# Attention, router and the first expert layer on one core: convolution weights loaded apart, router indices first, second-layer weights made at the end, attention order written out anew

## What is computed

```python
x = x + _L0_conv_ref(_ln_c(x), ...)      # attention: 8 heads, softmax over keys and queries
t = _to_tokens(x)
t = t + _L0_ffn_ref(_ln_t(t), ...)       # 8 experts, the router picks two per IMAGE
x = _from_tokens(t, x)
x = x + _L1_conv_ref(_ln_c(x), weight)   # 3x3 convolution with the signs of the weights
t = _to_tokens(x)
t = t + _L1_ffn_ref(_ln_t(t), ...)       # 8 experts, two per TOKEN
```

```python
logits = jnp.mean(x, axis=1) @ Wr + br
routing_weights = jax.nn.softmax(logits, axis=-1)
capacity = float(math.ceil(N * CAPACITY_FACTOR / E))
expected_loads = routing_weights.sum(axis=0) * (N / B)
scale = jnp.where(expected_loads > capacity, capacity / expected_loads, 1.0)
routing_weights = jax.nn.softmax(routing_weights * scale, axis=-1)
top_w, top_i = jax.lax.top_k(rw_tok, K)   # K = 2
top_w = jax.nn.softmax(top_w, axis=-1)
```

## Time and profile before

| | |
|---|---|
| median of 3 runs | 370.65 us (370.17 to 375.33) |
| profiled execution: span from first to last instruction | 370.4 us |
| the median less this span | 0.25 us |
| PE busy (share of the span) | 331.5 us (90%) |
| DVE busy | 264.2 us (71%) |
| ACT busy | 235.4 us (64%) |
| POOL busy | 95.8 us (26%) |
| attention, from the start to the first read of the token sums | 0 to 105.9 us |
| router, to the first copy of a selected weight | 105.9 to 115.4 us |

### The profile page before, as it was taken

One profiled execution on the slowest core, in us unless ns is written; L12 is line 12 of the kernel. 1 busy time (PEld: TensorE's weight loads), 2 busy tenths in 40 slices (PEclk: granted clock), 3 DMA queues, 4 the chain that ended last, 5 costly groups with the idle time before them and its releaser, 6 DMA issues.

```text
span 370.4 us, 5249 instructions
## 1 busy us (share of the span) xinstructions
PE 331.5 (90%) x1709; PEld 177.8 (48%) x1709; DVE 264.2 (71%) x532; ACT 235.4 (64%) x448; POOL 95.8 (26%) x83
## 2 busy tenths in 40 slices
PE   8967999999967676789999899999999899898994
PEld 6556787878943133443434344344344344243230
DVE  3466978789543447779778969969958959947862
ACT  3533767778635453567678659769759766656653
POOL 6224374664410112412005103103105103102000
PEclk9989999999988969699999999999999999999999
DMA  5961000000000000039192193193193095075573
GB/s 152 146 202 32 3 1 2 0 3 2 2 0 2 0 1 0 0 112 354 43 386 86 33 357 117 33 356 115 35 374 96 4 327 173 0 259 215 191 308 65
DMA packets 27724, 42.48 MB, mean 115 GB/s; under 512 B 15857, under 2 KB 17649, under 8 KB 27697
## 3 DMA queue, kind: packets, MB, share of 16 engines
q1 hardware_dynamic: 27696, 42.14, 36.1%
HBM read 39.25 MB, written 2.88 MB: 114 GB/s over the span
## 4 chain that ended last, share of the span: by engine, by line
PE 32%; DVE 27%; DMA 12%; issue 10%; POOL 7%; SPq 6%; ACT 4%; POOLq 1%; ACTq 0%; DVEq 0%
DMA GB<-spread 9%; POOL rstdA L545 5%; PE ps L800 5%; PE ps L911 4%; PE ps L722 4%; DVE HB L1311 3%; PE ps L678 3%; DVE varA L1202 2%; SPq L486 2%; DVE XC L1311 2%; PE ps L709 2%; PE ps L690 2%; DMA spread<-GT 1%; DVE XN L1207 1%; DVE XN L1209 1%
## 5 line engine op out<-in xcount | busy, mean ns | idle before, releaser
L800 PE MATMUL ps<-ET,W1B 64*128 64x512 f32 x256 | 69.0, 641 | 1.4 <-ACT HB L1521 1.4
L1311 DVE TENSOR_TENSOR HB<-HB,GB 128x1024 f32<-128x1024 f32 x44 | 53.1, 1221 | 17.6 <-DMA GB<-spread 13.7
L1521 ACT ACTIVATE HB<-ps,B1B 128x1024 f32<-128x1024 f32 x44 | 48.1, 1114 | 15.5 <-PE ps L800 15.1
L545 POOL TENSOR_TENSOR rstdA<-varA,pow_half 128x8 f32<-128x8 f32 x16 | 30.4, 1897 | 74.1 <-DVE varA L1202 74.1
L911 PE MATMUL ps<-HB,W2B 128*64 128x512 f32 x176 | 44.8, 608 | 0.9 <-DVE HB L1311 0.9
L545 POOL TENSOR_TENSOR rstdB<-varB,pow_half 128x8 f32<-128x8 f32 x8 | 14.9, 1865 | 112.4 <-DVE varB L1244 112.4
L800 PEld LDWEIGHTS ps<-ET,W1B 64*128 64x128 f32 x256 | 21.3, 189 | 29.0 <-issue 17.7
L545 POOL TENSOR_TENSOR rstd<-var,pow_half 128x4 f32<-128x4 f32 (+1 forms) x24 | 29.1, 1219 | 22.9 <-DVE var L1015 13.9
L1311 DVE TENSOR_TENSOR XC<-XC,GB 128x1024 f32<-128x1024 f32 x20 | 24.1, 1220 | 7.1 <-DMA GB<-spread 6.7
L849 PE MATMUL ps<-VP,WC 128*128 128x512 f32 x96 | 27.3, 428 | 0.7 <-ACT VP L1484 0.7
L560 POOL TENSOR_TENSOR QS<-QS,rqsum 128x512 f32<-128x512 f32 x16 | 17.0, 1060 | 30.2 <-DVE rqsum L1076 30.2
(11 more groups left out here) (225 smaller groups left out, 627.7 us busy)
## 6 DMA issues: line engine op xcount, KB each, us to landing
...
```

What stands on the lines that cost most here:

```text
L545: pool.tensor_tensor(out_, var, pow_half[:, 0:n], ALU.pow).then_inc(s[rstd_sem], 1)
L800: mm(ps[:, H_BANKS[n % 2][c], :], weights[half(c), :], tokens(half(c)), start=True, stop=True).then_inc(s["h"], 1)
L1311: tt(HG[b][e], HG[b][e], GB[:, e, :], ALU.mult).then_inc(s["f_hg"], 1)
L1521: av(HG[b][e], HID[n % 2], ACT.Gelu, bias=B1B[:, e:e + 1]).then_inc(s["gelu"], 1)
```

## The change

It has five parts.

1. **Convolution weights.** WCS gets a place of its own (slot 1 of HB, free until the second layer), and SP sends both loads right behind the images, with no wait between them. `set_conv` is split into `set_signs` and `set_scale`.
2. **Placement of one-off steps.** On DVE, `set_signs` goes from pair 0 to pair 3, `set_scale` and `set_layer1` behind the last `normalise2_`, directly ahead of the router; `set_fold` goes ahead of `order_rows`, `set_bo` behind `block_diagonal`. `set_second` goes from between `q_to_channels2` and `u_to_channels3:2` to behind the last `u_to_channels1` on PE, and behind the last `u_channels3` on ACT.
3. **Attention order.** `ATTENTION_PLAN` is replaced by the whole order written out (`ATTENTION`). On PE `queries3` comes after `xn_to_channels0` of the next pair, where it came ahead of `residual0`; `attend1` comes ahead of that `xn_to_channels0`; for pair 0 `q_to_channels0` comes ahead of `centre0:1`. The second layer's lists (`FIRST`, `PLAN`, `LAST`) are written out as one list, `LOOP`, with every part in the place that it had.
4. **Router.** The second softmax is no longer normalised before the two largest are sought: they are found as smallest of the negated scores, the scores being P1 times min(1, capacity / load). The indices have a column of their own in D2, a product of one row on PE, and IDX is cast from it before the weights are worked out. The product for the column sum takes the reciprocal of the softmax's sum as its weights, so it need not wait for P1. ACT has four small exponentials where it had three, and `gelu_table` is gone. `constant_products` stand 1, 4, 1 where they stood 2, 7, 1.
5. **`a_select`.** Both indices are loaded first, then W1S and B1S of both experts are copied, then W2S of both; for image 0 the last two wait for WI.

```diff
-            for dst, src, step, sig in ((WCstage, wconv, 0, "ld_conv"), (WCS, wcs, SET_SIGNS, "ld_conv")):
-                ge(sp, s["set_dve"], step)
-                sp.dma_start(dst, src).then_inc(s[sig], 16)
+            for dst, src in ((WCstage, wconv), (WCS, wcs)):
+                sp.dma_start(dst, src).then_inc(s["ld_conv"], 16)
             for dst, src in ((WR[:, :], wr), (BR[:, :], br), (W1A[:, :, :], w1a), (B1A[:, :], b1a),
...
-        WCS = W1stage[:, 0:5, :].rearrange("p a n -> p (a n)")[:, 0:C * TAPS]
+        WCS = HB[:, 1, 0:C * TAPS]
...
-            def set_conv(p, par):
-                vec.wait_ge(s["ld_conv"], 16)
+            def set_signs(p, par):
+                vec.wait_ge(s["ld_conv"], 32)
...
+            def set_scale(p, par):
                 vec.wait_ge(s["ld_conv"], 32)
...
-            constant_products(AT_BANK[1], 2)
-            pe.wait_ge(s["router_dve"], RD_P1)
-            rp.done(mm(r_ps[0:E, 0:E], ones[:, 0:E], R[:, 1, :], start=True, stop=True))
-            constant_products(AT_BANK[1], 7)
-            pe.wait_ge(s["router_dve"], RD_D2)
-            rp.done(mm(ps[:, UT_BANK, 0:4 * B], ones[:, :], D2[:, :, :].rearrange("p b k -> p (b k)"),
+            constant_products(AT_BANK[1], 1)
+            pe.wait_ge(s["router_dve"], RD_SUM1)
+            rp.done(mm(r_ps[0:E, 0:E], RV[:, 2, :].broadcast_to([E, E]), R[:, 1, :], start=True, stop=True))
+            constant_products(AT_BANK[1], 4)
+            pe.wait_ge(s["router_dve"], RD_D2I)
+            rp.done(mm(ps[0:1, UT_BANK, 0:2 * B], ones[:, 0:1], D2[:, 1].rearrange("p b k -> p (b k)"),
                        start=True, stop=True))
             constant_products(AT_BANK[1], 1)
+            pe.wait_ge(s["router_dve"], RD_D2W)
+            rp.done(mm(ps[:, UT_BANK, 2 * B:4 * B], ones[:, :], D2[:, 0].rearrange("p b k -> p (b k)"),
+                       start=True, stop=True))
...
+            vec.wait_ge(s["router_pe"], 3)
+            rd.done(vec.tensor_copy(IDX[:, :], ps[0:1, UT_BANK, 0:2 * B]))
...
-            av(gelu_table[:, :], R[:, 1, 0:1], ACT.Gelu)
...
-                for k in range(2):
-                    e = act.value_load(IDX[0:1, bass.ds(2 * b + k, 1)], min_val=0, max_val=E - 1)
+                picked = [act.value_load(IDX[0:1, bass.ds(2 * b + k, 1)], min_val=0, max_val=E - 1) for k in range(2)]
+                for k, e in enumerate(picked):
                     av(W1S[:, k], W1A[:, bass.ds(e, 1), :].rearrange("p a f -> p (a f)"), ACT.Copy)
                     av(B1S[:, k:k + 1], B1A[:, bass.ds(e, 1)], ACT.Copy).then_inc(s["a_sel"], 1)
+                if b == 0:
+                    act.wait_ge(s["router_dve"], RD_WI)
+                for k, e in enumerate(picked):
                     av(W2S[:, k, :], W2A[:, bass.ds(e, 1), :].rearrange("p a c -> p (a c)"), ACT.Copy,
```

252 lines of the change are left out of this document (117 added, 135 removed), and 111 rows, old and new, of tables (act, pe, pool, vec).

## The result

The changed kernel takes 366.24 us (median of 4, 364.17 to 367.48), the kernel before beside it 372.1 us (370.17 to 375.33). The ratio is 0.985, 95% interval 0.981 to 0.989. So the change wins 1.5 to 1.9%, 6 to 8 us where 10.3 were forecast, and 366.24 us lies above the range of 357.3 to 364.5. The ratios leave out two stray executions, one of e6 (417.49 us) and one of the kernel before beside e13 and e14 (1060.83 us).

A forecast was written before the change was run, and what follows sets the result against it. Steady attention was taken as bound by PE, gains lying before saturation, at attention's end and in the router: 6.0 + 1.7 + 2.6 = 10.3 us off the 370.4 us span, plus 0.25, gives 360.3 us; 8-in-10 range 357.3 to 364.5.

The forecast's parts named there:

- Early attention: Chain from block_diagonal to pair 1's second normalise1_, shortened by removed stalls and new order: 6.0 us won, bounds 4.6 and 6.9.
- rival of 3 times 1 us: Steady attention: the new order makes PE wait 1 us at q_to_channels3 in each of three pairs, 363.3 us; chance 0.17.
- Steady attention: Full pairs, bound by PE: later queries3 still leaves enough reserve, so 0 us lost, at most 1 us per pair.
- End of attention: Behind the last attend: set_second leaves saturated PE work for waits there, 1.7 us won, bounds 1.2 and 2.2.
- the two waits cover all of it but a few hundredths: End of attention: PE's waits of 1.09 and 0.81 us hide nearly all of set_second's 1.93 us.
- Router: From the token sums through index choice to expert layer: fewer instructions bring a_output 2.6 us sooner, bounds 0.9 and 3.3.
- The second index load: On ACT ahead of the first expert copy: one more value_load costs between 0.2 and 0.94 us, taken as 0.5.
- drain: At ACT's table load before the first Gelu: a drain costs 1.4 us more, 361.7 us; a rival, chance 0.04.
- I let the shift pass 1 to 1: Second layer: its lists are unchanged part for part, so time won before it reaches the end in full.
- 253: Sign to check: from the first Gelu to the end stay 253 us.
- main step: Said to be wrong if DVE reaches pair 1 no sooner than 28 us or the second layer takes other than 253.
- The 0.25 us around the span: Whole kernel: the median of the runs lies 0.25 us above the profiled span, added to 360.1 for 360.3 us.

The follow-up runs named there:

- e6: Changed kernel with ACT reading the second expert index behind the first expert's copies, not directly behind the first index: 364.23 us, ratio 0.980.
- e13: Changed kernel with DVE's f_gated5 placed behind a_zn instead of ahead of it in two places of the loop: 364.85 us, ratio 0.982.
- e14: Changed kernel with order_rows ahead of set_fold, set_second in two halves, r in two instructions and f_gated5 behind a_zn in two places: 363.17 us, ratio 0.978.
- e9: The changed kernel itself, unaltered, measured and profiled a second time: 364.15 us, ratio 0.981.
- e1: Changed kernel with order_rows back ahead of set_fold on DVE: 363.8 us, ratio 0.978.
- e10: Changed kernel with POOL's last four memsets waiting until both copies of order_rows are done: 364.08 us, ratio 0.982.
- e11: Changed kernel with the DVE instruction that makes r (32 x 2) issued as two of 32 x 1: 365.23 us, ratio 0.982.
- e2: Changed kernel with set_second back between attention steps, ahead of u_to_channels3:2, on PE and ACT, nearly its old place: 366.74 us, ratio 0.986.
- e7: Changed kernel with PE's set_second cut in two halves, one ahead of u_to_channels2:3, one behind it: 363.16 us, ratio 0.978.
- e8: Changed kernel with order_rows ahead of set_fold on DVE and set_second in two halves: 362.78 us, ratio 0.977.
- e12: Changed kernel with order_rows ahead of set_fold, set_second in two halves, the second index read later and r in two instructions: 362.75 us, ratio 0.975.

## Why the prediction was wrong

The forecast was 10.3 us faster, with a chance of 0.77 for more than 2%; measured were 6 to 8. The direction and the largest term held; the steps that failed are `set_fold` and the end of attention, and the 1.8 us around the span were taken as 0.25. By the landmarks of e9, in which no long execution blurs them, u8 comes 4.85 us sooner (forecast 7.7), z 7.21 (forecast 10.3), and the span is 8.1 us shorter.

- **Early attention, 6.0: right in size.** 5.06 at the second `normalise1_`, 6.05 with `order_rows` first (e1), and the end at 30.63 us where 30.6 was written. The chain was followed through the right links: in e1 BD ends at 22.61 us (22.3 was taken), `context_out` at 25.13 (24.7 to 25.3), M at 25.55 (25.1 to 25.7). Its durations alone add up to 29.8 or 30.4 us; the text rounds up at each link, and that happens to be the 0.3 us of handing over that e1 shows from M on. That PE stays bound in steady attention held too: 20.20 of 20.20 us, no rival of 3 times 1 us.
- **`set_fold`, not priced at all: 1.0 us lost.** The failed step is the part on early attention, which took the start as unchanged. The diff moves six DVE instructions ahead of `order_rows`, and no term has them. They meet POOL's memsets there (e1, e10).
- **Steady attention, 0: 0.7 us lost in pair 1.** The prediction looked at `queries3` alone. The new order brings r beside `qnorm`, and the shift of 5.06 becomes 4.34 by pair 3's first `attend`. e11 gives back 0.5 of it.
- **End of attention, 1.7: the step that failed most.** It gave 0.25 us (0.5 in e9). Two assumptions fell. The last `attend` was to come 1.9 us sooner and came 1.4: PE waits 0.61 us for U at 92.47. The 1.9 for `set_second` itself are there (e2), and the last pair loses 0.5 of them in the new order. And "the two waits cover all of it but a few hundredths": the second wait, 0.81 us, isn't free time; it is ACT's copy of the `u_to_channels` ahead of it, out of the one bank, and moves with it. So only the first wait covered anything, and 0.87 us went through to u8. Split over the two waits all but 0.33 us fits (e7).
- **Router, 2.6: 2.35 in e9, nearly right.** In the profile shown it is 2.05, with the clock at 0.51 and 0.64 between 110 and 114 us (1.00 in e9). The cast comes 5.79 us behind u8 instead of 5.2 (5.86 in e9). The working had PE take up the index product at once; four products of zeros at half clock stood ahead of it. In the kernels that reach this place with PE at full clock for a part of it (e1 and e8, 1.00 from 104 to 106 us) it is 5.04 and 5.18. The second index load was taken at 0.5 us and took 0.55. The first Gelu was to come 9.1 us behind u8 and comes 9.76 (9.83 in e9), 1.5 us sooner and not 2.2; from it to z it then takes 3.38 us in e9 where it was 4.28, which is more than the 0.4 us of the working and in part luck. The table load ended at 111.09 us and the Gelu began at 111.10: no drain shows here, and none ahead of the load, since the last copy ends at 109.79. By the Trainium skill, page "ScalarE: Activation LUTs", section "What ACT_TABLE_LOAD costs", a drain of about 1.38 us would come on top; the rows of both kernels speak against it.
- **"I let the shift pass 1 to 1": wrong for a single execution.** In the second layer a pow of POOL takes 2.01 or 3.15 us. The kernel before had the long one for unit 6 in its profile (e1 to e12 gain 0.7 to 1.4 us there), and the changed kernel had it in its profile too, with the fall of the clock behind it: shift 6.34 before, 4.81 after. From the first Gelu to the end it takes 254.6 us, and 251.3 in e9, where 253 was named with the remark that another time would make the prediction wrong in its main step.
- **The 0.25 us around the span is 1.8.** The sum should have ended at 361.9 us. That alone is 1.5 of the 5.9 us by which 360.3 missed 366.24. It doesn't touch the gain.

From 10.3 at z: 1.0 for the start, 0.7 for r, 1.2 for the end of attention and 0.25 for the router leave 7.15, and e9 has 7.21. Its other 0.9 us come in the second layer, where the profile of before had its long pow.

Open is what it would be worth to keep PE at full clock through the router: in every profile it is at 0.50 for a while between u8 and z, and the products of zeros that would keep PE busy stand in the way of the short ones. Also that the gains of e12 and e14 ahead of the router don't show in their medians wasn't followed to its end. Why the pow of unit 3 is always the long one, and that of unit 6 seldom, was not tried: the order on DVE is the same at both.
